# Audio tower on one core: split up-projection products, bands turned in DRAM, later small loads, a shorter GpSimd ending

## The reference

```
# 1 token layer
h = xf @ W_proj + b_proj                     # xf: 2048 x 1024
y = layernorm(h) * g + b
w = softmax(y @ W_wgen + b_wgen)             # 8 heads x 5 taps per token
conv[t] = sum_k w[t, head, k] * y[t - 4 + k] # causal, inside a sequence of 64
h = h + relu(conv @ W_ff + b_ff)
# 2 attention layer
h = h + attention(layernorm(h))              # 8 heads of 64, 64 tokens, causal
# 3 feed-forward layer, 16 heads of 64 channels, channels permuted by perm
t = layernorm(h)[:, perm].reshape(2048, 16, 64)
t = gelu(einsum('bhd,hdm->bhm', t, up))      # up:   16 x 64 x 256
t = einsum('bhm,hmd->bhd', t, down)          # down: 16 x 256 x 64
h = h + t[:, unperm]
```

## Time and profile before

| | |
|---|---|
| median of 3 runs | 983.7 us (983.49 to 984.62) |
| the profiled execution's own time | 982.39 us |
| its span in the profile | 980.7 us |
| TensorE busy | 956.6 us (98% of the span) |
| VectorE, ScalarE, GpSimd busy | 510.6, 425.8, 401.5 us |
| mean granted TensorE clock | 0.993 |

### The profile page before, as it was taken

How to read it: one execution, slowest core, us unless ns; L and a number is a source line. 1 busy time by engine, 2 the same in 40 slices (tenths; PEclk the granted TensorE clock), 3 DMA queues, 4 the chain that set the end, 5 groups by cost and what they waited for, 6 DMA issues and landing times.

```text
span 980.7 us, 15765 instructions
## 1 busy us (share of the span) xinstructions
PE 956.6 (98%) x6132; PEld 714.6 (73%) x6132; DVE 510.6 (52%) x841; ACT 425.8 (43%) x756; POOL 401.5 (41%) x324
## 2 busy tenths in 40 slices
PE   9999999999999999999999999999999999999996
PEld 7878787777777888788778878878887877533331
DVE  6253535868458312356475166156063567859451
ACT  6245454373544543446253243243132232467553
POOL 1225252444542112823560550551023288668632
PEclk9999999999999999999999999999999999999998
DMA  8651909096354264149003002100223966724521
GB/s 287 240 174 2 218 3 234 5 167 191 98 196 126 67 132 173 43 156 338 1 12 99 21 11 67 53 12 22 57 75 129 307 260 230 263 88 130 182 76 65
DMA packets 74920, 122.89 MB, mean 125 GB/s; under 512 B 29143, under 2 KB 38359, under 8 KB 70878
## 3 DMA queue, kind: packets, MB, share of 16 engines
q1 hardware_dynamic: 68686, 104.93, 36.3%
q0 software_dynamic: 5120, 16.78, 5.0%
q10 hardware_dynamic: 1040, 0.16, 0.1%
HBM read 79.36 MB, written 42.50 MB: 124 GB/s over the span
## 4 chain that ended last, share of the span: by engine, by line
PE 83%; POOL 5%; DVE 4%; issue 3%; DMA 2%; ACT 2%; POOLq 0%; SPq 0%; ACTq 0%; DVEq 0%
PE bank L333 21%; PE bank L335 20%; PE bank L334 20%; PE bank L1880 6%; PE bank L1889 6%; PE bank L1632 2%; POOL vacc L369 2%; POOL wf_l L327 2%; PE bank L1603 1%; POOL acc L397 1%; DVE sq L414 1%; PE bank L1762 1%; DMA hg<-h_s,rows 1%; PE bank L1789 1%; DVE h L1432 1%
## 5 line engine op out<-in xcount | busy, mean ns | idle before, releaser
L369 POOL TENSOR_TENSOR vacc<-vacc,sq 128x512 f32<-128x512 f32 x72 | 97.3, 1352 | 44.0 <-ACT sq L419 30.8
L333 PE MATMUL bank<-cv_h,wf_h 128*128 128x512 f32 x256 | 104.5, 408 | 0.0
L333 PE MATMUL bank<-xa_h,wp_h 128*128 128x512 f32 x256 | 102.6, 401 | 0.7 <-DVE xa_l L1154 0.7
L335 PE MATMUL bank<-xa_h,wp_l 128*128 128x512 f32 x256 | 100.3, 392 | 0.0
L334 PE MATMUL bank<-xa_l,wp_h 128*128 128x512 f32 x256 | 100.3, 392 | 0.0
L335 PE MATMUL bank<-cv_h,wf_l 128*128 128x512 f32 x256 | 100.0, 391 | 0.0
L334 PE MATMUL bank<-cv_l,wf_h 128*128 128x512 f32 x256 | 99.9, 390 | 0.0
L1135 ACT ACTIVATE gt<-bank 128x512 f32<-128x512 f32 x128 | 66.1, 603 | 53.0 <-PE bank L1880 53.0
L741 POOL TENSOR_TENSOR fo<-fo,res 128x512 f32<-128x512 f32 x32 | 42.8, 1351 | 106.0 <-ACT fo L887 76.6
L1880 PE MATMUL bank<-dd,up_f 64*128 64x512 f32 x256 | 63.6, 615 | 0.9 <-DVE h L1432 0.9
L1889 PE MATMUL bank<-gt,dn_f 128*64 128x512 f32 x256 | 61.8, 604 | 0.0
(11 more groups left out here) (180 smaller groups left out, 2184.2 us busy)
## 6 DMA issues: line engine op xcount, KB each, us to landing
xs<-x_t SPq DMA_DIRECT2D x32, 256.0 KB, 6.1
h_s<-ho SPq DMA_DIRECT2D x8, 1024.0 KB, 8.0
res<-h_s SPq DMA_DIRECT2D x32, 256.0 KB, 3.6
h_s<-fo SPq DMA_DIRECT2D x32, 256.0 KB, 2.4
dc<-h_s SPq DMA_DIRECT2D x4, 2048.0 KB, 8.7
h<-h_s SPq DMA_DIRECT2D x8, 1024.0 KB, 7.6
h_s<-h SPq DMA_DIRECT2D x8, 1024.0 KB, 4.8
band_s<-zero SPq DMA_DIRECT2D x4, 1072.0 KB, 8.3
```

The costliest lines, as they stand in the source:

```text
L333: pe.matmul(o, wh, xh, start=start, stop=False)
L335: return pe.matmul(o, wl, xh, start=False, stop=stop)
L369: g.tensor_tensor(vacc[:, :], t[:, 0, :] if k == 1 else vacc[:, :], t[:, at, :], ALU.add).then_inc(ln_vac, 1)
```

## The change

Four edits:

1. **Up products of the last two chunks.** For steps 16 to 31 the up product is made by three float32r matmuls per block and head, instead of one float32 matmul. ACT copies `up` to `up_h` in two halves (after the gelus of steps 5 and 6), DVE makes `up_l`; per step ACT makes `dd_h` (three steps ahead, a ring of 4 blocks) and DVE `dd_l`, in place of `dd`.
2. **Bands.** `wk5` is kept as [token, tap, (head, tile)], stored by ten DMAs of 64x32 elements per chunk in place of two, into a `band_s` whose innermost index is the unit; the skew is now a step of whole rows. The load is two DMAs in place of four, and what lands is already turned. The PE transposes of bands are gone; DVE's copy into `ar` now reads `band` in SBUF, with a stride of 32 elements.
3. **Small loads.** `vecs`, `perm` and `w_gen` are loaded by SP after the third block of the second half of `w_proj`.
4. **POOL's ending.** POOL's waits for the scatters are gone. SP's stay.

```diff
-                if k == 3:
+            for k in range(KB):
+                unit_load(sp, U_PROJ + KB + k)
+                if k == SMALL_AFTER:
                     sp.dma_start(vec[:, :], vecs).then_inc(const_ld, 16)
                     sp.dma_start(rows[:, :], perm).then_inc(const_ld, 16)
+                    sp.dma_start(wg_raw[:, :, :], w_gen.rearrange("(k p) n -> p k n", p=P)).then_inc(wg_ok, 16)
...
                 for s in range(2):
+                    for tap in range(TAPS):
+                        at = (s * SEQ_ROWS + tap) * LINE
+                        dst = band_s[n][at:at + SEQ * (LINE + UNITS)].rearrange("(q n) -> q n", q=SEQ)[:, 0:UNITS]
+                        sp.dma_start(dst, wk5[s * SEQ:(s + 1) * SEQ, tap, :]).then_inc(skewed, 16)
...
+                for s in range(2):
+                    at = (s * SEQ_ROWS + TAPS - 1) * LINE
+                    sp.dma_start(dst[s * SEQ:(s + 1) * SEQ, :, :],
+                                 band_s[n][at:at + SEQ * LINE].rearrange("(r n) -> r n", r=SEQ))\
+                      .then_inc(band_ld[n % 2], 16)
...
                 elif u == U_FF + 4:
-                    g.wait_ge(at_mm, 8)
+                    g.wait_ge(ar_ev, 8)
...
-            for k in range(KB):
-                g.wait_ge(d_st[k], 16 * CH)
...
-            act.dma_start(wg_raw[:, :, :], w_gen.rearrange("(k p) n -> p k n", p=P)).then_inc(wg_ok, 16)
...
+            def xd_high(b):
+                act.wait_ge(xd_sc, b + 1)
+                if b >= SPLIT_FROM + RING:
+                    act.wait_ge(up_mm, 4 * (b - RING) + 4)
+                act.activation(dd_h[:, b % RING, :], dd[:, b % KB, :], ACT.Copy).then_inc(xd_hi, 1)
...
+                if s in UP_AT:
+                    half = slice(4 * UP_AT.index(s), 4 * UP_AT.index(s) + 4)
+                    act.wait_ge(up_ld, 32)
+                    act.activation(up_h[:, half, :], up_f[:, half, :], ACT.Copy).then_inc(w_hi, 1)
+                if SPLIT_FROM <= s + RING - 1 < CH * KB:
+                    xd_high(s + RING - 1)
...
-            def band_evac(n, h):
-                since(v, at_mm, n, 8, h + 1)
+            def band_turn(n, h):
+                if h == 0:
+                    v.wait_ge(band_ld[n % 2], 32 * (n // 2 + 1))
+                if n == 0 and h == 0:
+                    v.wait_ge(a_mm, 8 * CH)
                 since(v, cv_mm, n, 8, h - 1)
-                v.tensor_copy(ar[:, h % 2, :], bank[AT_BANK][:, 0:N // 2]).then_inc(ar_ev, 1)
+                b = band0 if n == 0 else band
+                v.tensor_copy(ar[:, h % 2, :].rearrange("p (t q) -> p t q", q=SEQ),
+                              b[:, :, h * TILES:(h + 1) * TILES].rearrange("p q t -> p t q")).then_inc(ar_ev, 1)
...
+            def xd_low(b):
+                v.wait_ge(xd_hi, b + 1 - SPLIT_FROM)
+                v.tensor_tensor(dd_l[:, b % KB, :], dd[:, b % KB, :], dd_h[:, b % RING, :].bitcast(F32),
+                                ALU.subtract).then_inc(xd_lo, 1)
...
-                if h % 4 == 0:
-                    pe.wait_ge(band_ld[n % 2][h // 4], 32 * (n // 2 + 1))
-                if h >= 1:
-                    pe.wait_ge(ar_ev, 8 * n + h)
-                elif n > 0:
-                    pe.wait_ge(ff_ev, 8 * (n - 1) + AT_BANK + 1)
-                for u in range(TILES // 2):
-                    mm = pe.transpose(bank[AT_BANK][:, u * P:(u + 1) * P], b[:, h * TILES // 2 + u, :],
-                                      ident[:, :])
-                mm.then_inc(at_mm, 1)
...
+                else:
+                    for j, r in enumerate(halves):
+                        pe.matmul(bank[2 * blk + j][:, :], up_h[r, a, cols], dd_h[r, b, :], start=True, stop=False)
+                    for j, r in enumerate(halves):
+                        pe.matmul(bank[2 * blk + j][:, :], up_h[r, a, cols], dd_l[r, a, :], start=False, stop=False)
+                    for j, r in enumerate(halves):
+                        mm = pe.matmul(bank[2 * blk + j][:, :], up_l[r, a, cols], dd_h[r, b, :], start=False, stop=True)
...
+RING, SPLIT_FROM, UP_AT = 4, 16, (5, 6)
```

More of the change, by code:

```diff
@@ L113, in audio_tower @@
         ar = place("ar", [P, 2, N // 2], F32, E + 8 * KIB)
-        band = place("band", [P, UNITS // 2, P], F32, E + 16 * KIB)
+        band = place("band", [P, SEQ, UNITS], F32, E + 16 * KIB)
         yr_h = place("yr_h", [P, 2, N], F32R, E + 32 * KIB)
@@ L152, in audio_tower @@
         up_f = place("up_f", [P, KB, FF_MID], F32, R1)
+        up_h = place("up_h", [P, KB, FF_MID], F32R, R1 + 8 * KIB)
+        up_l = place("up_l", [P, KB, FF_MID], F32R, R1 + 16 * KIB)
+        dd_h = place("dd_h", [P, RING, N], F32R, STAGE)
+        dd_l = place("dd_l", [P, KB, N], F32R, R2 + 48 * KIB)
         dn_f = place("dn_f", [P, KB * FFB, FF_IN], F32, R1 + 32 * KIB)
@@ L1493, in _ @@
                     d_add((s - 1) // KB, (s - 1) % KB)
+                if SPLIT_FROM <= s + 2 < CH * KB:
+                    xd_low(s + 2)
+                if s - 1 in UP_AT:
+                    up_low(UP_AT.index(s - 1))
                 n, k = divmod(s - PREP_AFTER, KB)
```

71 lines of the change are left out of this document (36 added, 35 removed).

## The result

| | before | after |
|---|---|---|
| median | 983.6 us (982.26 to 984.62, 4 runs) | **972.24 us** (971.0 to 974.9, 4 runs) |
| ratio | | 0.9884, 95% interval 0.9862 to 0.9906 |
| the profiled execution, its span | 982.39, 980.7 us | 974.9, 973.1 us |
| TensorE busy | 956.6 us | 948.4 us |

The change makes the kernel 11.4 us faster (1.2%); 971.0 us was predicted. The profiled execution of after is the slowest of its four and has the lowest mean granted clock of them (0.989, the others 0.991 to 0.996).

A forecast was written before the change was run, and what follows sets the result against it. TensorE, busy 98% of the span, was taken as the bound. Terms 5.8 + 4.3 + 0 + 0.7 + 1.9 = 12.7 us less gave 971.0 us from the median 983.7; range 966.5 to 976.8, the forecast's own 967 to 974.

The forecast's parts named there:

- Up products, 5.8 forecast: Feed-forward steps 16 to 31: an up product takes 1.56 us instead of 1.92, 16 x 0.36 = 5.8 us less.
- The sign of being wrong altogether: Steps 16 to 31: PE waiting for `dd_l` or a gelu would mean that ACT or DVE sets the step.
- Band transposes, 4.3 forecast: Convolution, chunks 1 to 3: 24 heads x 0.22 = 5.2 us, less 0.9 for waits; between 3.5 and 5.2.
- Chunk 0, 0 forecast: Chunk 0's convolution: 1.7 us saved on transposes, 1.8 lost to copy collisions; 0, between 3 less and 4 more.
- the bound on the good side: Chunk 0's convolution: up to 3 us less, including PE's stalls without a releaser, which may go with the small packets.
- Band DMAs, 0: SP's ten stores per chunk: 0.42 us per issue, 4.2 us against 2.82, landing sooner; nothing on the path, 0.
- The start, 0.7: First product: without `w_gen` ahead, x lands about 1 us earlier; 0.7 us less, between 0 and 0.9.
- The end, 1.9: Program end: without the waits POOL's drain starts 2.0 us earlier and takes as long; 1.9 us less.
- The rival in which it follows the landing: Program end: POOL's drain ends a fixed time after the landing, so nothing is gained there; 972.9 us, no chance given.
- Halves one after the other: Up products: half-height float32r matmuls don't overlap; 2.92 us each, +16.0 us instead of -5.8, 992.8 us; 6%.
- weight loads as the pace: Up products: pairs overlap but take 0.29 us for two loads; 1.94 us each, the 5.8 gone, 976.8 us; 11%.
- The copy collides: Chunk 0's convolution: DVE's copy waits for POOL at most heads; 4.8 us more, 975.8 us; 13%.

The follow-up runs named there:

- alone: The kernel before with only the split up products of steps 16 to 31: 979.59 us, 0.9951 of before.
- POOL late: The changed kernel with POOL's first four weight splits held until chunk 0's last token transposes, to test the copy collision: 976.59 us, 0.9923 of before.
- again: The changed kernel run once more, unchanged, for a second profile: 974.55 us, 0.9895 of before.
- small loads alone: The kernel before with only the later loads of the small tensors: 983.21 us, 1.0006 of before.
- The kernel with ten stores: The kernel before with each of its two band stores per chunk cut into five, pieces still 20 bytes: 983.47 us, 1.0007 of before.
- the kernel with two stores: The changed kernel with a chunk's ten band stores put into two, and the attention stage's load issued two output blocks earlier: 972.18 us, 0.9893 of before.
- the split from 12: The changed kernel with the split up products from step 12 on in place of 16: 973.96 us, 0.9904 of before.

## Why the prediction was right, point by point

**The bound.** Right: TensorE was busy for 97% of the span, and every gain came from its queue or its waits.

**Up products, 5.8 forecast.** The mechanism is right and the size a little off. The term that was mis-sized is the pair at the pace of the full-height stream, 6 x 0.2265 + 0.20 = 1.56 us. It is 0.235 us a pair and 1.60 us in all, so a step takes 3.46 on average and not 3.43: from the `d_add` of step 16 to that of step 31 it is 54.71 us before and 50.15 after, 4.6 less over the 14 up products in between. That is 0.33 a product and 5.2 for 16, in place of 5.8. There is also a wait that I had costed at nothing. In step 14 ACT holds back the gelus for its copy into `dd_h` (DVE, POOL and ACT, after):

```profile
895.07 2.28 DVE L1473 TENSOR_TENSOR dd<-hg,mtd 128x512 f32<-128x512 f32 x1
...
895.52 2.96 POOL L373 TENSOR_TENSOR vacc<-vacc,sq 128x512 f32<-128x512 f32 x2
...
897.39 1.64 DVE L1492 TENSOR_TENSOR dd<-dd,rtd 128x512 f32<-128x512 f32 x1
...
899.07 0.63 ACT L1134 ACTIVATE dd_h<-dd 128x512 fp32r<-128x512 f32 x1 [1.91 <-DVE dd L1492]
```

The two DVE operations are 2.28 and 1.64 us beside POOL, not 0.68 each, and the step takes 4.16 in place of 3.79 (0.37 us). "The copies run three and two steps ahead, so their latency is covered" was wrong in the one place where their input is late. It cost nothing in the end: in the three profiles that have the split and no stretch of half clock there (alone, POOL late and again) this step and the next together take 9.19 us, against 9.52 before, which is again 0.33 less.

The sign of being wrong altogether, a wait for a gelu in steps 16 to 31, is absent from the profile of after, but not from all others. In the second profile of the same kernel PE stands for 0.64 us without a releaser and then here:

```profile
922.27 0.50 PE L1913 MATMUL bank<-dd_h,up_h 64*128 64x512 f32 x2 [1.14 <-ACT gt L1141]
```

The split alone has the same two waits, and POOL late one of 1.36 us. Each has it once, and ACT itself had stood idle for 2.09 us ahead of it (2.5 in POOL late), so ACT doesn't set the pace of these steps. What stopped both engines there is open.

**Band transposes, 4.3 forecast.** The gain itself was under-stated: chunks 1 to 3 became 4.8 us shorter (136.79 to 132.02), and 24 x 0.22 is 5.2. But the 0.9 that I took off for waits was too little. A head of chunk 1, later in the timeline of after, has the forecast spacing, 0.53 us from the transposes to the convolution where it was 0.75:

```profile
265.12 0.60 PE L1637 MATMUL bank<-ident,db_next 128*128 128x128 f32 x4
265.65 0.56 PE L1656 MATMUL bank<-ar,yt 64*64 64x64 f32 x22
```

Against it stand the longer wait for the ReLU at chunk 1 (0.85 to 2.07 us, some 0.8 of which is in the table's fourth row), and the wait for `dc` that takes 1.9 us ahead of the attention stage. I had looked for late inputs within the chunks and not at the stage behind them. A wait that is just met before is the first to open when PE arrives earlier.

**Chunk 0, 0 forecast.** The two terms of the forecast don't balance. Less its stalls the old loop takes 13.2 us in the kernel with the split alone (14.09 with a stall of 0.94), 13.2 with the small loads alone and 13.5 before; the new one takes 13.97. The waits for `ar` went from 0.3 to 2.5 us, more than the 1.7 that the transposes gave, so the loop would be 0.4 to 0.8 us longer. What made it shorter is the bound on the good side, which has come true: the stalls without a releaser are in the timelines of all six kernels with old bands, somewhere from 214 to 224 us, 0.9 to 3.8 us in sum. They are in none of eight with new bands but for one of 0.21 us. The kernel with ten stores of 20-byte pieces has the most, 3.81 us, so the number of stores is not what removes them; the piece size or the loads remain, and these were not separated. Through this before loses 3.2 us that after doesn't, of which the first wait of chunk 1 takes up a part. From the end of the token products to that convolution it is 53.79 before and 51.84 after, 2.0 less in place of 0, inside the range that I gave.

**Band DMAs, 0.** Right. A store of 8 KB lands after 2.3 us in after (one of 40 KB after 4.5 in the kernel with two stores), against 11.5 before; the packets fell from 74920 to 53800. An issue was 0.62 us and not 0.42, so ten are 6.2 us, and still PE has no wait between the convolutions of chunks 1 and 3.

**The start, 0.7.** Right within what the profiles can tell: 0.6 us.

**The end, 1.9.** Right, 2.0 us, and "as long as before" is not quite how it works. The sequencer's row at the end of after (ns, start):

```profile
L47 POOLq DRAIN  x1: 6506/6506/6506, 966.4 to 966.4; - x1
```

POOL's last issue is 966.60 to 967.57 us (L810), so the drain begins inside it and ends at 972.87, 5.3 us behind the issue's end. It was 5294 ns when POOL had waited for the landing first, and so ended 7.4 us behind the issue. The rival in which it follows the landing fell: SP saw the landing at 969.4, and it took no notice.

**What the sum missed.** Ahead of the attention stage 1.9 us, in the output projection 1.1 (the collision); the stalls of chunk 0 gave back 2.0. The two profiles differ by 7.6 us, and after has three stretches of half clock more, in chunks 1 to 3, in the output projection and in the feed-forward stage. One of them costs 1.64 us there by two kernels with the old up product (from the `d_add` of step 13 to the last, 69.66 us with one in small loads alone, 68.02 without in before). With the stretches taken out the table gives 5.4 (feed-forward) + 4.8 (bands) + 2.0 (chunk 0 with its stalls, net of the wait at chunk 1) + 0.9 (start) - 0.2 (token products) + 2.0 (end) - 1.9 - 1.1 = 11.9 us, against 11.4 in the medians with an interval of 9.2 to 13.6. The sum of 12.7 came as near as it did because errors of both signs were in it: that part of the agreement is luck.

**The rivals.** Halves one after the other (2.92 us for an up product), and weight loads as the pace (1.94): measured 1.60. The copy collides: true in its mechanism, 2.5 us of waits for `ar` in place of the 4.8 that it was given (1.3 of them shown by the test), since three copies of eight were on PE's path and not all.

## What to carry to other kernels

When PE becomes faster in one stage, list the waits ahead that were only just met, the next stage's first load above all; here 1.9 us of 4.8 went there, and an issue two blocks earlier removes the wait. DVE operations with SBUF sources that share a stage with POOL take 0.4 to 0.7 us or 0.8 to 2.3 us, by who starts first; cost them at the long value wherever something on PE's path follows them. And with changes of 0.2% compare stage by stage between profiles, after marking the stretches of half clock, since the medians alone can't tell.

## What the runs showed of the hardware that was not expected

- **Row halves overlap** side by side in the queue and three matmuls apart, at 0.235 us for a float32r pair of 512 columns; with float32 a pair takes 0.43 us.
- **Who starts first decides.** DVE's first `vs_l` gave PE its operand after 0.84 us when it started with POOL's sum, and after 1.70 us when 0.26 us behind. In all six profiles with the long pause POOL had started first, in none of the other eight. The Trainium skill (SBUF — State Buffer, "SBUF: two separate sides") calls the shared port pair an exclusive lock, held for a whole instruction by whichever engine starts first; the trace agrees, in five places: chunk 0's copies, `vs_l`, the inputs of step 14, `dd_l` in the split from 12, and the centerings beside it.
- **POOL's drain** ends 5.3 us after the end of its last indirect DMA's issue when POOL doesn't wait for the landing, and takes 5.3 us behind the wait when it does (7.4 us after the issue), so the wait is paid in full.
- **Half clock.** Stretches of 3.4 us at the 1.2 GHz level come in different places in two profiles of one program, and each costs up to 1.7 us (1.64 measured in the feed-forward stage).
- **PE stalls without a releaser** in the first convolution were there with 20-byte band pieces, in all six profiles, and gone with 128-byte ones. The cause was not isolated.
